# One 1024-column sum of squares behind K's square, in place of two of 512, in a pipelined attention and FFN kernel

## The reference

```
def l2norm(t):
    return t / jnp.maximum(jnp.linalg.norm(t, axis=-1, keepdims=True), 1e-12)
...
for i in range(DEPTH):          # 6
    qkv = shift_tokens(x) @ Wqkv[i]
    q = l2norm(q) * q_scale;  k = l2norm(k) * k_scale      # per head of 64
    q = q * cos * scale + rotate_half(q) * sin * scale
    k = k * cos / scale + rotate_half(k) * sin / scale
    x = local_attention(q, k, v) @ Wo[i] + x
    x = ffn_layer(shift_tokens(x), ...) + x
```

## Time and profile before

| | |
|---|---|
| median of 3 runs | 1734.22 us |
| lowest and highest | 1728.39, 1739.47 us |
| the profiled execution, its own time | 1738.27 us |
| its span in the trace | 1736.5 us |
| mean granted TensorE clock | 0.967 |

### The profile page before, as it was taken

The page is one execution under the profiler, slowest core; times in us unless marked ns, Lnnn a source line. Parts: engine busy times, 40 slices in busy tenths (PEclk is TensorE's granted clock), DMA queues, the critical chain, the costliest instruction groups (busy, mean ns, idle before and its releaser), DMA issues.

```text
span 1736.5 us, 67874 instructions
## 1 busy us (share of the span) xinstructions
PE 1532.5 (88%) x28560; PEld 1223.3 (70%) x28656; DVE 1360.1 (78%) x2564; ACT 1244.8 (72%) x4601; POOL 1264.0 (73%) x1492
## 2 busy tenths in 40 slices
PE   6589989899998899999889998989999989989985
PEld 5367777677777677777667777767777767777774
DVE  4678888878887977877878787787788787887873
ACT  3267868777877777777777777786776777776773
POOL 2378787777877867867767768787778687887770
PEclk8699999999999999999999999999999999999998
DMA  4012211021211111211111212111211112111011
GB/s 120 1 40 57 57 40 52 27 58 33 67 57 35 45 47 45 67 45 47 33 28 57 67 38 60 33 40 46 57 51 47 47 33 57 27 49 45 27 45 31
DMA packets 50878, 80.62 MB, mean 46 GB/s; under 512 B 8947, under 2 KB 16806, under 8 KB 50574
## 3 DMA queue, kind: packets, MB, share of 16 engines
q1 hardware_dynamic: 50574, 76.28, 15.8%
HBM read 18.62 MB, written 1.05 MB: 11 GB/s over the span
## 4 chain that ended last, share of the span: by engine, by line
PE 63%; ACT 12%; DVE 11%; issue 7%; POOL 7%; DMA 0%; SPq 0%; POOLq 0%; DVEq 0%
PE ps L442 9%; PE ps L389 7%; PE ps L396 7%; ACT pr L650 7%; PE ps L412 6%; PE ps L452 6%; PE ps L391 5%; PE ps L390 5%; PE ps L423 4%; PE ps L483 4%; DVE v L956 2%; ACT sq L613 2%; PE ps L406 2%; POOL t L779 2%; POOL t L798 2%
## 5 line engine op out<-in xcount | busy, mean ns | idle before, releaser
L779 POOL TENSOR_TENSOR t<-t 128x512 f32<-128x512 f32 x384 | 486.2, 1279 | 84.2 <-DVE t L951 83.6
L650 ACT ACTIVATE pr<-ps,nmax 128x64 f32<-128x64 f32 x1536 | 460.6, 353 | 0.9 <-DVE nmax L966 0.9
L798 POOL TENSOR_TENSOR t<-t,rn 128x512 f32<-128x512 f32 x384 | 397.6, 1056 | 7.5
L650 ACT ACTIVATION_READ_ACCUMULATOR pr<-ps,nmax 128x1 f32 x1536 | 376.8, 248 | 0.0
L949 DVE TENSOR_TENSOR t<-ps,rope 128x512 f32<-128x512 f32 x384 | 261.6, 681 | 58.1 <-PE ps L396 37.9
L809 POOL TENSOR_TENSOR pr<-pr,rsum 128x512 f32<-128x512 f32 x192 | 200.8, 1046 | 135.1 <-DVE rsum L973 134.4
L389 PE MATMUL ps<-w_hi,xt_hi 128*128 128x512 f32 x576 | 272.7, 473 | 26.7 <-DVE t L951 10.3
L613 ACT ACTIVATE sq<-ps 128x512 f32<-128x512 f32 x384 | 233.3, 622 | 69.9 <-PE ps L391 63.2
L951 DVE TENSOR_TENSOR t<-ps,rope 128x512 f32<-128x512 f32 x384 | 260.7, 679 | 0.0
L931 DVE TENSOR_REDUCE ss<-sq 128x8 f32<-128x512 f32 x384 | 259.2, 675 | 0.7
L390 PE MATMUL ps<-w_lo,xt_hi 128*128 128x512 f32 x576 | 235.0, 408 | 3.0 <-issue 3.0
(11 more groups left out here) (122 smaller groups left out, 2714.0 us busy)
## 6 DMA issues: line engine op xcount, KB each, us to landing
v_win<-v SPq DMA_DIRECT2D x384, 128.0 KB, 2.3
wqkv<-wqkv_in SPq DMA_DIRECT2D x36, 256.0 KB, 3.9
xsh<-xr SPq DMA_DIRECT2D x24, 224.0 KB, 2.6
wo<-wo_in SPq DMA_DIRECT2D x6, 512.0 KB, 3.8
w<-w_in SPq DMA_DIRECT2D x6, 342.0 KB, 4.6
w<-w_in SPq DMA_DIRECT2D x6, 172.5 KB
x<-x_in SPq DMA_DIRECT2D x4, 256.0 KB, 4.1
out<-x SPq DMA_DIRECT2D x4, 256.0 KB, 2.7
```

Of the source, the lines that this page charges most:

```text
L650: i = A(pr[:, c, odd * SPAN:(odd + 1) * SPAN], ps[:, S_BANK[odd], c * SPAN:(c + 1) * SPAN], ACT.Exp, bias=nmax[:, odd, c:c + 1], accum_out ...
L779: G.tensor_tensor(t1[:, c, :], t1[:, c, :], t2[:, c, :], ALU.add).then_inc(qk_added[c], 1)
L798: G.tensor_tensor(w, w, rn[:, par(u), h2, a, :].unsqueeze(2).broadcast_to([P, 8, E]), ALU.mult).then_inc(done, 1)
```

## The change

`sum_squares` now takes the pair of chunks of a half, which lie side by side in `sq`: one reduce over 1024 columns into 16 numbers. It is called only behind the rotation of K1 and behind that of K0, and the calls for Q1 and Q0, which stood behind the rotation of Q1 and behind `add_residual`, are gone. One semaphore belongs to a half, not one to a chunk.

```
             def sum_squares(u, c):
-                V.tensor_reduce(ss[:, par(u), c // 2, c % 2, :], sq[:, c, :].rearrange("p (h e) -> p h e", h=8), AX.X,
-                                ALU.add).then_inc(ss_ready[c], 1)
+                h2 = c // 2
+                V.tensor_reduce(ss[:, par(u), h2].rearrange("p a h -> p (a h)"),
+                                sq[:, 2 * h2:2 * h2 + 2, :].rearrange("p a (h e) -> p (a h) e", h=8), AX.X, ALU.add).then_inc(ss_ready[h2], 1)
...
                 run(s, 0, rotary, Q1)
                 run(s, 0, lower_w, Q1)
-                run(s, 0, sum_squares, Q1)
                 run_quad(s, 8, ffn_lower)
                 run_quad(s, 9, ffn_gated, 2)
                 run(s, 2, inverse_sum, 1)
                 run(s, 3, add_residual)
-                run(s, 0, sum_squares, Q0)
                 run(s, 0, rotary, K1)
                 run_quad(s, 9, ffn_residual)
                 run(s, 0, sum_squares, K1)
                 run(s, 0, rotary, K0)
                 run_input(s, 9, lower_xt)
                 run(s, 0, sum_squares, K0)
                 run(s, 0, clamp_norm)
```

More of the change, by code:

```diff
@@ L167, in build @@
     qkv_ps = sems("qkv_ps", 6)
-    sq_ready, ss_ready, rope_done, qk_added, tq_ps, tq_ready = (
-        sems(s, 4) for s in ("sq_ready", "ss_ready", "rope_done", "qk_added", "tq_ps", "tq_ready"))
+    ss_ready = sems("ss_ready", 2)
+    sq_ready, rope_done, qk_added, tq_ps, tq_ready = (
+        sems(s, 4) for s in ("sq_ready", "rope_done", "qk_added", "tq_ps", "tq_ready"))
     ss_clamped, ln_done, rn_guess, rn_ready, s_ps, max_ready, o_ps = (
@@ L930, in sum_squares @@
             def sum_squares(u, c):
-                V.tensor_reduce(ss[:, par(u), c // 2, c % 2, :], sq[:, c, :].rearrange("p (h e) -> p h e", h=8), AX.X,
-                                ALU.add).then_inc(ss_ready[c], 1)
+                h2 = c // 2
+                V.tensor_reduce(ss[:, par(u), h2].rearrange("p a h -> p (a h)"),
+                                sq[:, 2 * h2:2 * h2 + 2, :].rearrange("p a (h e) -> p (a h) e", h=8), AX.X, ALU.add).then_inc(ss_ready[h2], 1)
             def clamp_norm(u):
-                for c in range(4):
-                    if c in (Q0, K0):
-                        dve.wait_ge(ss_ready[c], u + 1)
+                for h2 in range(2):
+                    if h2 == 0:
+                        dve.wait_ge(ss_ready[h2], u + 1)
                 w = ss[:, par(u)].rearrange("p b a h -> p (b a h)")
```

## The result

| | before | after |
|---|---|---|
| median of 5 runs | 1735.15 us | 1754.94 us |
| lowest to highest | 1728.39 to 1740.81 | 1749.31 to 1760.64 |
| profiled execution | 1738.27, span 1736.5 | 1749.31, span 1747.5 |

The ratio is 1.0107, with a 95% interval of 1.0067 to 1.0147: **slower by 19.8 us**, 1.1%. 1740 had been forecast, in a range up to 1753. The profiled execution of after is the lowest of its five, and that of before is above its median, so the two traces show only 11 us of the difference. Part of that goes with TensorE's clock: its mean granted value was 0.967 in the profiled execution of before and 0.969 in that of after, the highest of after's five runs, whose other four had 0.961 to 0.966.

A forecast was written before the change was run, and what follows sets the result against it. K1's rotation on VectorE was taken as gated by TensorE and ScalarE, with Q's sums filling a hole. Terms 13.5 - 3.4 + 1.3 - 3.0 - 2.3 = +6.1 us on 1734.22 gave 1740 us, range 1726 to 1753.

The forecast's parts named there:

- the hole: VectorE's idle before K1's rotation, filled by Q's two sums; to grow to about 1.2 us a step, some 100 in all.
- the gate: K1's rotation on VectorE waits for K1's square (TensorE and ScalarE); the clamp behind it would start 1.07 us later.
- the norm steps: Steps with the FFN norm, 17 counted: late clamp, FFN operations and copies of V delay TensorE, 13.5 us (7.5 to 19.6).
- One reduce at 1.13: A 1024-column sum on VectorE taken as 1.13 us, against 1.19 for two of 512; bounds 1.07 and 1.19.
- Steps with GpSimd's last addition gated: GpSimd's last addition waits for VectorE and holds the clamp, which ends some 0.57 us late, not 1.07; cost nothing.
- What takes some of it back: TensorE's 69.9 us of "issue" waits before value matmuls shrink after later starts; a quarter of 13.5 taken, -3.4 us.
- I take half: Norm steps: half of up to 1.0 us for the last FFN operation caught behind GpSimd's normalisation; 1.75 us late in all.
- (a): Ends of five layers: VectorE's second inverse of the sums comes sooner for GpSimd, 0.6 us x 5 = -3.0 us.
- (b): FFN residual step: hT's last third could start 0.13 us sooner, 18 waits of TensorE, -2.3 us.
- the fill: Pipeline fill, counted with the FFN residual steps: 0.54 and twice 0.2 to 0.5, together +1.3 us.
- GpSimd's ring: Slower rival: GpSimd's late Newton step delays its queued work; 1750 to 1763 us, chance 0.17, of which 0.12 beyond 1%.
- Its worst norm steps: Upper bound for the norm steps, everything 2.2 us late: 19.6 us summed over the 17.

The follow-up runs named there:

- the spare sum: Unused 1024-column sum added to the kernel before in the norm steps: ratio 1.0026 behind the FFN norm, 1.0092 ahead of the clamp, 1.0273 behind the clamp.

## Why the prediction was wrong, point by point

- **What bounds the kernel, the hole, the gate.** Right. The clamp came 1.10 us later behind the first copy of V in the norm steps (16 intervals: 11.23 to 12.33), where 1.07 had been said. The row on squares grew to 62.1 us, and a further 28 us of the hole opened in front of the second inverse of the softmax sums; some 70 us, not 100. K1's rotation starts within 0.3 us behind the end of K1's square in 86 units of the trace before, not 88, which changes nothing.
- **One reduce at 1.13, 11.5 us of busy time saved and worth nothing.** Right. A wide sum starts 1.13 us ahead of its neighbour (799.44 and 800.57 in the step above).
- **Steps with GpSimd's last addition gated.** The mechanism was right. These rows of POOL and DVE answer to the earlier trace rows:

```profile
787.43 1.27 POOL L780 TENSOR_TENSOR t<-t 128x512 f32<-128x512 f32 x1 [0.92 <-DVE t L954]
...
788.51 0.22 DVE L942 TENSOR_SCALAR ss<-ss 128x32 f32<-128x32 f32 x1
...
790.94 1.39 DVE L959 COPY v<-ps 128x512 f32<-128x512 f32 x2 [1.07 <-PE ps L392]
```

  The clamp ends with GpSimd's addition and loses half of its delay. But "cost nothing" was a little wrong: these intervals are 3.3 and 5.5 us longer in the sum of 16. In the two traces without the change in the norm steps they are 1.8 and 2.8 longer.
- **The norm steps, 13.5 us.** Right in place and kind, too small: 15.0 and 17.1 us in the two traces. The clamp was as late as worked out (1.10, and 0.23 more of being held). The mis-sized term is "I take half": the four operations take 2.14 us together in nearly all of these steps, where it was mostly 1.24, so 0.9 more and not 0.5. I had also left out who else waits. TensorE's transposes of the FFN input stand in front of Q0's projection and wait for them themselves.
- **"What takes some of it back", -3.4 us.** This step failed. TensorE's nameless waits are 69.9 us before and 71.6 and 73.5 after, no shorter for a later start, and 74.5 with the spare sum behind the clamp, where TensorE is latest. I had inferred a supply that runs on, from no row. The intervals right behind the norm steps are indeed 3.6 and 4.2 us shorter in sum, but TensorE stood 6 us less at its lower clock in them, which by itself is worth about 3.
- **The gains (a) and (b), -5.3 us, and the fill, +1.3.** This step failed by more than the others. The waits went as said, the time did not. At the layer's end GpSimd waits

```profile
866.85 1.04 POOL L810 TENSOR_TENSOR pr<-pr,rsum 128x512 f32<-128x512 f32 x1 [0.74 <-DVE rsum L976]
```

  which is 0.59 less than the 1.33 of the earlier trace rows, and the waits for hT in front of the down projection are nearly gone. Yet the kernel with the change in all but the norm steps is 4 us above the kernel before, twice, where these terms add up to 4 below. The 2 to 3 us of the steps of the earlier trace rows in those kernels are part of it. What the rest is stays open; the intervals of those two runs are 4 us wide to either side.

In sum, two steps of the prediction failed: it booked shorter waits as time won (-5.3 us, where the steps outside the norm steps cost +4 and not -4), and it counted on TensorE's nameless waits to take 3.4 us back, which they did not. The half catch was the right mechanism at too small a size, by 2 to 4 us. Together these make 13 to 15 us, near the 13.7 between the forecast 6.1 and the measured 19.8. The terms are from different runs, whose noise is 4 us each, so that the sum fits is in part luck; and the prediction had no term for TensorE's clock, with which some 5 us of the whole go by the estimate above. In whole runs the norm steps alone cost 12 us (8 to 16), less than the 15.6 us that their intervals are longer in that trace.

The rival that ends slower, GpSimd's ring, was the wrong mechanism: of the places of the spare sum, one that leaves the ring's start alone is the dearest. The range ended 2 us below the median. Its worst norm steps (19.6) with nothing taken back and no gains would have reached 1755, so the two failed steps are what it lacked.

## What to carry to other kernels

Before merging two instructions, look at what each of them fills. A sum that runs while its engine would wait is free. Behind the gate it delays everything queued after it by its whole length, and the kernel pays where no idle covers that. When a change shifts a list of instructions by a microsecond, check for each that shares a port with another engine what it now runs beside, and check the shift at every place at once: the same 1.13 us cost 4.5, 16 or 47 us depending on where it stood in one list. Look at the granted clock beside every such number: here the dearest place also had the lowest clock. And a nameless wait in the trace is not slack to be counted on.

## What the runs showed of the hardware that I had not expected

- Small VectorE operations with two SBUF inputs beside a row of GpSimd instructions get through about one for each of them. Four that take 1.24 us in the clear took 3.57 beside three normalisations. By the Trainium skill ("SBUF — State Buffer", section "Who interferes with whom") a VectorE instruction with two SBUF inputs contends with a GpSimd instruction that reads SBUF, and the later one is blocked until the other ends. The trace agrees: in the traces of before, of after and with the spare sum, operations of the FFN norm longer than 0.45 us all end 0.15 us after an instruction of GpSimd, and a reduce in their place takes 268 to 286 ns, never more.
- An instruction that nobody had looked at met the same. `ffn_lower` (L1014, after L1017), two SBUF inputs, 512 columns, went from 943 to 1175 ns in the mean when the sum of Q1 ahead of it was gone. It then starts 0.6 us earlier beside an instruction of GpSimd that is already running, and in both kernels it mostly ends 0.55 us after that one. The mean is 1112 to 1224 in the other kernels without that sum, 709 to 916 in those with it. That the hole covered it here is likely, not shown.
